# Balancing two batches' 4x4 matrices in one pass of doubled width

## The chip, the core and the metric

The kernel runs on one core of a Trainium2 chip. Its engines are named as in the profile: PE (TensorE; PEld is its weight load), DVE (VectorE), ACT (ScalarE), POOL (GpSimd) and SP (SyncE, which issues DMAs). Each engine runs its own list of instructions in order and waits on semaphores for the others. The metric is the device time of one execution in microseconds; three runs of the kernel before gave a median of 1330.84 us.

## What is computed

Four layers on x of shape (2, 512, 512): 2 batches of 512 tokens with 512 channels. Each layer is

```
xn = layernorm(x)
x  = x + attention_layer(xn) * silu(other_layer(xn))
```

The kernel cuts each batch into four tiles of 128 tokens (T = 512 columns). The attention of layers 0, 2 and 3 has 32 heads of 16, that of layer 1 eight heads of 32; layer 2 is not causal. The part that matters here is the other branch of layer 1. Per token it makes a 4x4 matrix from a projection and balances it (Sinkhorn, 50 rounds), then mixes four streams of 128 channels with it:

```
u = -logsumexp(Z + v, axis=-1)     # rows      } 50 times
v = -logsumexp(Z + u, axis=-2)     # columns   }
H_res = exp(Z + u + v);  H_res = (1 - g) * I + g * H_res
x_mixed = einsum('btij,btjc->btic', H_res, x_streams)
```

The kernel works on exp(Z) and divides by row sums and column sums in turn. One batch has 4 tiles of 128 tokens on the 128 partitions, so its matrices are 4 x 16 = 64 columns of float32, and the sums 16 columns.

## The kernel before

Up to 312 us there are phases of their own: the first normalisation, the projection of layer 0 and its low-rank feed-forward. From there on everything is one woven part (function weave). It is made of stages, each a list of ticks, and a tick issues a few instructions on several engines. Stages stand in strands by letter: a holds the attentions (batch 0 and 1 of layer 0, then of layer 1, 2, 3), b the chain between them (outward product, gate and add, normalise, project, lead of the next attention), c the lead of batch 1's first attention, s the layer-1 branch (class Streams, two stages s0 and s1 for the two batches), r the routed branches of layers 2 and 3, w the splitting of weights on POOL. The string TURNS says in which order the ticks of the strands follow each other ("s12 a" is twelve ticks of s, then one of a), and merge writes one order from it; every engine's list follows that order. Within a strand the order is fixed.

The names in the rows: w_banks are seven PSUM banks that all stages share; w_qs and w_ks hold stacked queries and keys; w_mx the row maxima of the scores (L1402, made by PE at L1259, L1263 and L1271); w_pr the probabilities (scores at L1299, exponentials at L1345, masked on POOL at L1384); w_po the sums over values (L1317); a group of four heads (two in layer 1) ends with L1327, L1410 and L1413. L982, L1008, L667, L1014, L1021 and L1026 are the outward product, its gate and its addition; L718 to L739 the normalisation, L667 and L883, L909 the projection.

Streams has ticks 0 to 12 for logits and exponentials, 13 to 21 for the branch that sums the streams and multiplies by W_branch (L1831 to L1838), 22 to 321 for the balancing (one DVE instruction each, six to a round), three ticks for the gate and 16 for the mixing (L1867, 64 instructions per batch). The balancing steps wait for one another through one semaphore; they read and write columns of w_region. s1 stands behind s0 in its strand, so batch 0's balancing lies under batch 1's first attention and the stages behind it, batch 1's under the layer-1 attentions and the beginning of layer 2's. Batch 0's outward product of layer 1 needs s0's result for its gate, batch 1's needs s1's.

Of the kernel before, what the change touches and what calls it, by code (L numbers as in the profile page):

```python
# [30 lines left out]
P = 128  # L31
D = 512
# [1643 lines left out]
class Streams(Stage):  # L1676


    N, ITERS, INV_TAU, EPS = 4, 50, 10.0, 1.1920929e-07

    def __init__(self, g, b, xn, w24, wb, base, gate, norm, weights):
        self.g, self.b, self.xn, self.w24, self.wb, self.base, self.gate = g, b, xn, w24, wb, base, gate
        self.norm, self.weights = norm, weights
        s = g.signals
        self.squared, self.meaned, self.rooted = s.take("h_squared", NI), s.take("h_meaned", 1), s.take("h_rooted", 1)
        self.gate_exped, self.made = s.take("h_gate_exped", 1), s.take("h_made", 1)
        self.done = s.take("h_done", 13)
        self.centred, self.exped = s.take("h_centred", 2), s.take("h_exped", 2)
        self.balanced = s.take("h_balanced", 6 * self.ITERS)
        self.pre, self.turned, self.hi, self.lo = s.take("h_pre", NI * 4), s.take("h_turned", 1), s.take("h_hi", 1), s.take("h_lo", 1)  # L1690
        self.branched, self.kept = s.take("h_branched", 1), s.take("h_kept", 1)
        self.posted, self.mixed, self.silued = s.take("h_posted", NI), s.take("h_mixed", NI * 16), s.take("h_silued", NI // 2)
        self.pre_at, self.bal_at = 13, 22
        self.gate_at = self.bal_at + 6 * self.ITERS
        self.mix_at = self.gate_at + 3
        self.ticks = range(self.mix_at + NI * 4 + 1)
        self.fills = {}

    def cost(self, t):
        if self.bal_at <= t < self.gate_at:  # L1700
            return 0.28
        return 1.0
# [40 lines left out]
    def act(self, act, t):  # L1743
        g, n = self.g, self.N
        if t < NI:
            act.wait_ge(self.norm.normed.sem, self.norm.normed.at + NI)
            if t == 0:
                wait_pos(act, self.posted.sem, self.posted.at)
                act.activation(g.h_gt[:, 0:1], self.gate, ACT.Exp, scale=-1.0).then_inc(self.gate_exped.sem, 1)
            wait_pos(act, self.squared.sem, self.squared.at + t)  # L1750
            act.activation(g.h_sq[:, :], self.xn[:, t, :], ACT.Square, accum_out=g.h_ss[:, t:t + 1]).then_inc(self.squared.sem, 1)
        if t == 5:
            act.wait_ge(self.meaned.sem, self.meaned.at + 1)
            act.activation(g.h_ss[:, :], g.h_ss[:, :], ACT.Sqrt).then_inc(self.rooted.sem, 1)
        if t == 11:
            act.wait_ge(self.centred.sem, self.centred.at + 2)
            act.activation(g.h_mix[:, :, :], g.h_mix[:, :, :], ACT.Exp, scale=self.INV_TAU).then_inc(self.exped.sem, 1)
            act.activation(g.h_pp[:, :, :], g.h_pp[:, :, :], ACT.Exp).then_inc(self.exped.sem, 1)
# [10 lines left out]
        if t - self.mix_at in (-1, 3, 8, 9):  # L1769
# [3 lines left out]
            for k in range(n):  # L1773
                op = act.activation(g.h_om[:, i % 2, k * P:(k + 1) * P], g.h_sq[:, i * P:(i + 1) * P], ACT.Copy,
                                    scale=g.h_pp[:, i, n + k:n + k + 1])
# [7 lines left out]
    def dve(self, dve, t):  # L1783
        g, n = self.g, self.N
        done = self.done
        if t == 4:
            dve.wait_ge(self.squared.sem, self.squared.at + NI)
            dve.tensor_scalar(g.h_ss[:, :], g.h_ss[:, :], 1.0 / D, self.EPS, ALU.mult, ALU.add).then_inc(self.meaned.sem, 1)
        res = g.h_lg[:, :, 0:n * n].rearrange("p t (i j) -> p t i j", j=n)
        two = g.h_lg[:, :, n * n:].rearrange("p t (i j) -> p t i j", j=n)  # L1790
        two_p = g.h_pp[:, :, :].rearrange("p t (i j) -> p (t i) j", j=n)
        if t == 6:
            dve.wait_ge(self.rooted.sem, self.rooted.at + 1)
            dve.reciprocal(g.h_rr[:, :], g.h_ss[:, :]).then_inc(done.sem, 1)
        elif t == 7:
            dve.wait_ge(self.made.sem, self.made.at + 1)
            dve.wait_ge(done.sem, done.at + 1)
            dve.tensor_tensor(g.h_lg[:, :, :], g.banks.at(self.fills["logits"])[:, 0:NI * 24].rearrange("p (t n) -> p t n", n=24),
                              g.h_rr[:, :].unsqueeze(2).to_broadcast([P, NI, 24]), ALU.mult).then_inc(done.sem, 1)
        elif t == 8:  # L1800
            dve.wait_ge(done.sem, done.at + 2)
            dve.tensor_tensor(g.h_lg[:, :, :], g.h_lg[:, :, :], self.base.unsqueeze(1).to_broadcast([P, NI, 24]),
                              ALU.add).then_inc(done.sem, 1)
        elif t == 9:
            dve.wait_ge(done.sem, done.at + 3)
            dve.tensor_reduce(g.h_m4[:, :], res, AX.X, ALU.max).then_inc(done.sem, 1)
            dve.tensor_reduce(g.h_m2[:, :, :], two, AX.X, ALU.max).then_inc(done.sem, 1)
        elif t == 10:
            dve.wait_ge(done.sem, done.at + 5)
            dve.tensor_tensor(g.h_mix[:, :, :].rearrange("p t (i j) -> p t i j", j=n), res,  # L1810
                              g.h_m4[:, :].rearrange("p (t i) -> p t i", i=n).unsqueeze(3).to_broadcast([P, NI, n, n]),
                              ALU.subtract).then_inc(self.centred.sem, 1)
            dve.tensor_tensor(g.h_pp[:, :, :].rearrange("p t (i j) -> p t i j", j=n), two,
                              g.h_m2[:, :, :].unsqueeze(3).to_broadcast([P, NI, 2, n]), ALU.subtract).then_inc(self.centred.sem, 1)
        elif t == 12:
            dve.wait_ge(self.exped.sem, self.exped.at + 2)
            m2 = g.h_m2[:, :, :].rearrange("p t i -> p (t i)")
            dve.tensor_reduce(m2, two_p, AX.X, ALU.add).then_inc(done.sem, 1)
            dve.wait_ge(done.sem, done.at + 6)
            dve.reciprocal(g.h_i2[:, :], m2).then_inc(done.sem, 1)  # L1820
            dve.wait_ge(done.sem, done.at + 7)
            dve.tensor_tensor(two_p, two_p, g.h_i2[:, :].unsqueeze(2).to_broadcast([P, NI * 2, n]), ALU.mult)\
                .then_inc(done.sem, 1)
        elif self.pre_at <= t < self.pre_at + 4:
# [497 lines left out]
```

## Time and profile before

| | us |
|---|---|
| median of 3 runs (1326.19 to 1334.57) | 1330.84 |
| the profiled execution | 1323.33 |
| its span in the profile | 1321.3 |
| busy PE, DVE, ACT, POOL | 1063.8, 862.6, 581.8, 328.6 |

The span is what the profile shows between the first and the last instruction. Busy times overlap between engines, so they are compared with the span, stage by stage, and not added.

### The profile page before, as it was taken

The numbers are of one execution on the slowest core, as the hardware profiler recorded it, in microseconds if no ns is written. First come the engines' busy times: TensorE is split into PE (matmuls) and PEld (weight loads), VectorE is DVE, ScalarE is ACT, GpSimd is POOL, SyncE is SP. The second block draws the span as 40 slices with busy tenths as digits, with TensorE's granted clock in tenths as the row PEclk, the third lists the DMA queues.
The fourth block names the chain that finished last, engine by engine and source line by source line (L and its number), as shares of the span: only waits on it lengthen the run. The fifth ranks groups of instructions, "written<-read, shape, count | busy, mean of one in ns | idle before, by whom it ended". The sixth has DMA issues, their size and how long they took to land.

```text
span 1321.3 us, 20167 instructions
## 1 busy us (share of the span) xinstructions
PE 1063.8 (81%) x7480; PEld 446.7 (34%) x7480; DVE 862.6 (65%) x1775; ACT 581.8 (44%) x801; POOL 328.6 (25%) x516
## 2 busy tenths in 40 slices
PE   3899999996779677756758666588889987999878
PEld 2444444442234322424323111232223343434424
DVE  5322221003567789989798999957978687757764
ACT  3433333001564643315533366555665666444562
POOL 2145444004653111101121000158310042111230
PEclk9889999997799768878979599788999998999999
DMA  8322220004110001100202000033102111220200
GB/s 314 117 72 72 72 72 0 0 0 104 51 43 17 13 13 31 60 13 15 71 28 79 19 19 19 17 113 111 47 23 82 48 45 34 61 73 29 66 14 32
DMA packets 54901, 69.74 MB, mean 53 GB/s; under 512 B 9526, under 2 KB 43444, under 8 KB 54800
## 3 DMA queue, kind: packets, MB, share of 16 engines
q1 hardware_dynamic: 50828, 58.57, 14.2%
q0 software_dynamic: 3984, 9.98, 2.7%
q8 instruction: 56, 0.92, 0.3%
q14 instruction: 33, 0.27, 0.1%
HBM read 49.45 MB, written 18.82 MB: 52 GB/s over the span
## 4 chain that ended last, share of the span: by engine, by line
DVE 33%; PE 30%; ACT 5%; issue 4%; DMA 3%; SPq 2%; POOL 0%; DVEq 0%; ACTq 0%
DVE w_mx L1402 15%; PE w_banks L667 9%; PE w_po L1317 7%; PE w_banks L1299 4%; PE w_banks L1271 3%; ACT w_pr L1345 2%; PE w_banks L1259 2%; DVE w_region L1867 2%; DVE w_region L1889 2%; PE w_banks L1327 2%; PE w_banks L1553 2%; DMA stack_scratch<-sl_region 1%; DVE w_region L1886 1%; DVE att L1021 1%; DVE w_region L1884 1%
## 5 line engine op out<-in xcount | busy, mean ns | idle before, releaser
L1345 ACT ACTIVATE w_pr<-w_banks 128x1024 f32<-128x1024 f32 (+1 forms) x312 | 313.8, 1014 | 301.9 <-PE w_banks L1299 301.2
L1402 DVE TENSOR_REDUCE w_mx<-w_banks 128x2 f32<-128x1024 f32 (+3 forms) x352 | 373.4, 1082 | 110.0 <-PE w_banks L1271 108.7
L1384 POOL TENSOR_SCALAR_AFFINE_SELECT w_pr<-w_pr 128x512 f32<-128x512 f32 (+1 forms) x184 | 109.2, 595 | 447.0 <-ACT w_pr L1345 446.7
L1299 PE MATMUL w_banks<-w_qs,w_ks 49*128 49x512 f16 (+7 forms) x832 | 134.3, 350 | 64.8 <-ACT w_pr L1345 30.2
L1271 PE MATMUL w_banks<-w_ks,w_qs 48*128 48x512 f16 (+7 forms) x832 | 143.0, 359 | 25.3 <-DVE w_mx L1402 21.8
L78 PE MATMUL f_pp<-xt,sl_region 128*128 128x512 f16 x672 | 149.5, 383 | 2.4 <-POOL sl_region L504 2.4
L1317 PE MATMUL w_po<-w_pr,w_vz 128*17 128x512 f32 (+7 forms) x1152 | 144.2, 538 | 2.1 <-ACT w_ou L1367 2.1
L1259 PE MATMUL w_banks<-mask_half,ident_half 64*128 64x128 bf16 (+1 forms) x768 | 68.6, 259 | 42.9 <-DVE w_mx L1402 25.5
L480 DVE TENSOR_TENSOR sl_region<-sl_region,f_pp 128x512 f32<-128x512 f32 x28 | 19.3, 688 | 120.6 <-ACT sl_region L495 120.6
L78 PEld LDWEIGHTS f_pp<-xt,sl_region 128*128 128x128 f16 x672 | 65.2, 99 | 84.0 <-issue 6.1
L1299 PEld LDWEIGHTS w_banks<-w_qs,w_ks 49*128 49x128 f16 (+1 forms) x832 | 40.8, 99 | 122.1 <-ACT w_pr L1345 55.7
L78 PE MATMUL d_pf<-f_wd,f_dt 128*128 128x512 f16 x336 | 74.3, 385 | 3.7 <-PEq L69 3.7
L1271 PEld LDWEIGHTS w_banks<-w_ks,w_qs 48*128 48x128 f16 (+1 forms) x832 | 47.7, 103 | 86.7 <-DVE w_mx L1402 49.0
L667 PE MATMUL w_banks<-xt,w_region 128*128 128x512 f16 x288 | 70.3, 391 | 5.6 <-DVE w_mx L1402 2.7
L1259 PEld LDWEIGHTS w_banks<-mask_half,ident_half 64*128 64x128 bf16 x768 | 29.3, 99 | 96.0 <-issue 57.1
L667 PE MATMUL w_banks<-w_wo,w_ot 128*128 128x512 f16 x192 | 49.3, 409 | 8.8 <-DVE w_ot L1008 8.8
L1317 PE MATMUL w_po<-w_pr,vz 128*17 128x256 f32 (+3 forms) x512 | 54.9, 508 | 1.2 <-POOL w_pr L1384 0.8
L1442 POOL DMA_DIRECT2D w_stage<-in_L_w x40 | 22.2, 556 | 133.1 <-issue 125.0
L1889 DVE RECIPROCAL w_region<-w_region 128x16 f32<-128x16 f32 x200 | 50.0, 250 | 4.9
L2219 DVE MEMSET w_po<- 128x512 f32 x1 | 0.5, 485 | 78.5 <-PEq L351 78.5
L511 POOL TENSOR_TENSOR f_dt<-sl_region,f_dt 128x512 f32 (+1 forms) x28 | 32.4, 1156 | 69.4 <-ACT f_dt L497 69.4
L78 PEld LDWEIGHTS d_pf<-f_wd,f_dt 128*128 128x128 f16 x336 | 33.2, 99 | 44.8 <-issue 6.3
(223 smaller groups left out, 1487.8 us busy)
## 6 DMA issues: line engine op xcount, KB each, us to landing
stack_scratch<-sl_region SPq DMA_DIRECT2D x102, 128.0 KB
w_qs<-stack_scratch SPq DMA_DIRECT2D x96, 96.0 KB, 2.3
sl_region<-in_L_gu SPq DMA_DIRECT2D x14, 512.0 KB
w_stage<-in_L_w POOLq DMA_DIRECT2D x36, 128.0 KB, 2.4
sl_region<-in_L_down SPq DMA_DIRECT2D x14, 256.0 KB
stack_scratch<-p_qk SPq DMA_DIRECT2D x24, 128.0 KB
w_ks<-stack_scratch SPq DMA_DIRECT2D x32, 96.0 KB, 2.6
bw_stage<-in_L_w SPq DMA_DIRECT2D x4, 640.0 KB, 9.9
```

What stands on the lines that cost most here:

```text
L78: mm = pe.matmul(out, left(a, c), right(b, c), start=first and k == 0, stop=last and k == n - 1)
L511: pool.tensor_tensor(dt[:, 1, ds(i, 1), b * T:(b + 1) * T], sd[:, b:b + 1, :], dt[:, 0, ds(i, 1), b * T:(b + 1) * T], ALU.subtract).then_i ...
L667: mm = pe.matmul(out, left(a, c), right(b, c), start=k == 0, stop=k == len(terms) - 1)
L1259: mm = pe.matmul(out[:, :, keys - P:keys], g.ident_half[64 * half:64 * half + 64, piece, :], g.mask_half[64 * half:64 * half + 64, piece, ...
L1271: mm = pe.matmul(out, g.qs[base:base + self.rows, slot, place, i * P:(i + 1) * P], g.ks[base:base + self.rows, k_slot, k_place, 0:keys], s ...
L1299: mm = pe.matmul(g.banks.pair_at(f)[:, half, at:at + T - q0], g.ks[base:base + self.rows + 1, k_slot, k_place, j * P:(j + 1) * P], g.qs[ba ...
L1317: mm = pe.matmul(g.po[s * a.sw:s * a.sw + a.hd + 1, q0:T], self.vz[:, j, head * a.kv // a.h, :], g.probs.at(self.pr_fill[og * self.n_u + u ...
L1327: mm = pe.transpose(g.banks.at(self.out_fill[og])[:, i * P:(i + 1) * P], g.ou[:, (self.base + og) % 2, i * P:(i + 1) * P], g.ident[:, :])
L1345: act.activation(g.probs.at(self.pr_fill[s])[:, :, 0:width], g.banks.pair_at(self.s_fill[s])[:, :, 0:width], ACT.Exp, scale=self.a.scale). ...
L1384: pool.affine_select(out=diagonal, in_=diagonal, compare_op=ALU.is_ge, fill=0.0, base=0, pattern=pattern, channel_multiplier=-1).then_inc( ...
L1402: dve.tensor_reduce(out, g.banks.pair_at(self.m_fill[m])[:, :, 0:heads * keys].rearrange("q h (p k) -> q h p k", k=keys), AX.X, ALU.max).t ...
L1889: op = dve.reciprocal(inverse, sums)
```

## The change

The balancing is taken out of Streams and becomes a stage of its own (class Balance) that works on both batches: h_mix becomes one tile of 2 x 64 columns, the sums and inverses one of 32, and each of the 300 instructions reads or writes twice the columns. There are 50 rounds in place of two times 50. It begins when both batches' exponentials are there. The strand s now is: s0 to its tick 21, s1 to its tick 12, the balancing, s0's gate and mixing, then s1's branch, gate and mixing. The small tiles of Streams and its semaphores get one copy per batch, and TURNS is a new table for the new strands.

```diff
-    def balance(self, dve, k):
-        g, n = self.g, self.N
-        byrow = g.h_mix[:, :, :].rearrange("p t (i j) -> p (t i) j", j=n)
-        bycol = g.h_mix[:, :, :].rearrange("p t (i j) -> p t j i", j=n)
+class Balance(Stage):
+    def __init__(self, g, streams):
+        self.g, self.streams, self.steps = g, streams, 6 * Streams.ITERS
+        self.balanced = g.signals.take("h_balanced", self.steps)
+        self.ticks = range(self.steps)
...
+    def dve(self, dve, t):
+        g, n = self.g, Streams.N
+        both = g.h_mix[:, :, :, :].rearrange("p b t m -> p (b t) m")
+        byrow = both.rearrange("p t (i j) -> p (t i) j", j=n)
+        bycol = both.rearrange("p t (i j) -> p t j i", j=n)
         sums, inverse = g.h_m4[:, :], g.h_i4[:, :]
-        if k > 0:
-            dve.wait_ge(self.balanced.sem, self.balanced.at + k)
-        step = k % 6
+        if t == 0:
+            for stage in self.streams:
+                dve.wait_ge(stage.exped.sem, stage.exped.at + 2)
+        else:
+            dve.wait_ge(self.balanced.sem, self.balanced.at + t)
+        step = t % 6
         if step == 0:
             op = dve.tensor_reduce(sums, byrow, AX.X, ALU.add)
         elif step == 2:
-            op = dve.tensor_tensor(byrow, byrow, inverse.unsqueeze(2).to_broadcast([P, NI * n, n]), ALU.mult)
+            op = dve.tensor_tensor(byrow, byrow, inverse.unsqueeze(2).to_broadcast([P, NT * n, n]), ALU.mult)
         elif step == 3:
             op = dve.tensor_reduce(sums.rearrange("p (t j) -> p t j", j=n), bycol, AX.X, ALU.add)
         elif step == 5:
             op = dve.tensor_tensor(bycol, bycol, inverse.rearrange("p (t j) -> p t j", j=n).unsqueeze(3)
-                                   .to_broadcast([P, NI, n, n]), ALU.mult)
+                                   .to_broadcast([P, NT, n, n]), ALU.mult)
         else:
             op = dve.reciprocal(inverse, sums)
         op.then_inc(self.balanced.sem, 1)
...
 TURNS = """
...
-    a2 w2 a2 w6 l w2 a2 w a14 w a w a3 w a2 w a2 w2 a w a10 w a2 w2 a w a2 c2 a c3 w a c a3 w c2 a3 c a c a c a c w2
+    w4 a3 w6 a w a12 w a3 w2 a3 w2 a10 w2 a5 w2 a4 w2 a w a2 c a w c w c w c2 l a c a2 c a c2 a3 c a2 c w a w c w a2
...
-                   "s": [all_of(s0), all_of(s1)], "r": [all_of(x) for x in (r20, r21, r30, r31)]}
+                   "s": [some_of(s0, 0, s0.gate_at), some_of(s1, 0, s1.pre_at), all_of(balance),
+                         some_of(s0, s0.gate_at, s0.ticks[-1] + 1), some_of(s1, s1.pre_at, s1.ticks[-1] + 1)], "r": [all_of(x) for x in (r20, r21, r30, r31)]}
```

The first place is DVE where the balancing begins. Before, batch 0's rounds begin there, among the maxima (L1402) of batch 1's first attention:

```order
L1838 TENSOR_TENSOR w_region<-w_banks,w_region 128x512
L1880 TENSOR_REDUCE w_region<-w_region 128x16
L1889 RECIPROCAL w_region<-w_region 128x16
L1882 TENSOR_TENSOR w_region<-w_region 128x64
L1884 TENSOR_REDUCE w_region<-w_region 128x16
L1889 RECIPROCAL w_region<-w_region 128x16
L1886 TENSOR_TENSOR w_region<-w_region 128x4x4x4
```

Now, with the same operations at other lines (L1893 to L1902), behind batch 1's exponentials:

```order
L1817 RECIPROCAL w_region<-w_region 128x8
L1819 TENSOR_TENSOR w_region<-w_region 128x32
L1893 TENSOR_REDUCE w_region<-w_region 128x32
L1902 RECIPROCAL w_region<-w_region 128x32
L1895 TENSOR_TENSOR w_region<-w_region 128x128
L1897 TENSOR_REDUCE w_region<-w_region 128x32
L1902 RECIPROCAL w_region<-w_region 128x32
L1899 TENSOR_TENSOR w_region<-w_region 128x8x4x4
```

Every row has twice the columns, and the first of them has moved from among batch 1's first attention to behind its normalisation.

The second place is DVE near the end of the balancing and behind it. Before, batch 1's last rounds stood among the maxima of layer 2's attention for batch 0:

```order
L1402 TENSOR_REDUCE w_mx<-w_banks 128x2
L1880 TENSOR_REDUCE w_region<-w_region 128x16
L1889 RECIPROCAL w_region<-w_region 128x16
L1882 TENSOR_TENSOR w_region<-w_region 128x64
L1402 TENSOR_REDUCE w_mx<-w_banks 128x2
L1884 TENSOR_REDUCE w_region<-w_region 128x16
L1889 RECIPROCAL w_region<-w_region 128x16
L1402 TENSOR_REDUCE w_mx<-w_banks 128x2
L1886 TENSOR_TENSOR w_region<-w_region 128x4x4x4
L1402 TENSOR_REDUCE w_mx<-w_banks 128x2
```

Now that attention's first maxima stand behind the projection (L883, L909) and the last mixes (L1862, which was L1867), with no balancing among them:

```order
L883 SCALAR_TENSOR_TENSOR sl_region<-w_banks,bw_cols,sl_region 128x512 x3
L909 TENSOR_TENSOR w_vz<-w_banks,bw_rows 128x32x16
L1862 SCALAR_TENSOR_TENSOR w_region<-sl_region,w_region 128x128 x32
L1592 COPY w_r_l<-w_banks 128x16
L1402 TENSOR_REDUCE w_mx<-w_banks 128x2 x12
L1592 COPY w_r_l<-w_banks 128x16
L1402 TENSOR_REDUCE w_mx<-w_banks 128x2
```

The layer-2 attention has moved from beside the balancing to behind it. Between the first and the last balancing step DVE now has 37 other instructions: 21 maxima (L1402), four pairs of L1410 and L1413, four L883, two L909 and two L1008, all of layer 1.

## Rows read from the trace of the kernel before

**Rows 1.** The page, busy us, share of the span, instructions.
```profile
PE 1063.8 (81%) x7480; PEld 446.7 (34%) x7480; DVE 862.6 (65%) x1775; ACT 581.8 (44%) x801; POOL 328.6 (25%) x516
```
**Rows 2.** Windows: stretch and length, busy us by engine, granted clock, DMA share, GB/s.
```profile
312.70:411.70 99.00, 74.84 (x827) 30.60 (x827) 63.76 (x76) 49.00 (x59) 62.87 (x123) 0.84 0.24 64
465.00:720.00 255.00, 183.31 (x1250) 85.10 (x1250) 224.41 (x717) 96.45 (x147) 40.52 (x69) 0.82 0.12 38
720.00:846.00 126.00, 76.93 (x455) 18.91 (x456) 120.03 (x291) 64.35 (x85) 1.35 (x3) 0.82 0.07 20
846.00:909.00 63.00, 50.76 (x337) 19.93 (x335) 43.79 (x69) 37.41 (x48) 38.38 (x70) 0.92 0.32 96
909.00:1060.00 151.00, 136.16 (x867) 45.46 (x866) 118.32 (x157) 88.05 (x113) 28.55 (x53) 0.98 0.19 56
1060.00:1318.00 258.00, 229.06 (x2009) 100.39 (x2007) 177.94 (x280) 129.53 (x164) 54.97 (x99) 0.98 0.15 44
```
**Rows 3.** Groups by line and form on DVE: count, busy us, mean ns, idle before.
```profile
L1889 DVE RECIPROCAL w_region<-w_region 128x16 f32<-128x16 f32 x200 | 50.0, 250 | 4.9
L1886 DVE TENSOR_TENSOR w_region<-w_region 128x64 f32<-128x64 f32 x100 | 27.0, 270 | 2.7
...
L1882 DVE TENSOR_TENSOR w_region<-w_region 128x64 f32<-128x64 f32 x100 | 23.4, 234 | 2.6
...
L1802 DVE TENSOR_TENSOR w_region<-w_region,w_base 128x96 f32<-128x96 f32 x2 | 0.5, 259 | 0.1
...
L1810 DVE TENSOR_TENSOR w_region<-w_region 128x64 f32<-128x64 f32 x2 | 0.4, 224 | 0.1
...
L1820 DVE RECIPROCAL w_region<-w_region 128x8 f32<-128x8 f32 x2 | 0.4, 204 | 0.1
...
L1794 DVE RECIPROCAL w_region<-w_region 128x4 f32<-128x4 f32 x2 | 0.4, 178 | 2.7 <-ACT w_region L1754 2.7
```
**Rows 4.** Timeline of DVE: start us, us, line, operation.
```profile
565.82 0.27 DVE L1886 TENSOR_TENSOR w_region<-w_region 128x64 f32<-128x64 f32 x1
...
567.51 0.27 DVE L1886 TENSOR_TENSOR w_region<-w_region 128x64 f32<-128x64 f32 x1
...
605.22 8.49 DVE L1867 SCALAR_TENSOR_TENSOR w_region<-sl_region,w_region 128x128 f32<-128x128 f32 x32
```
**Rows 5.** The chain that ended last, first attention: start us, us, what.
```profile
338.44 2.37 DVE w_mx L1402 x2
...
350.16 2.37 DVE w_mx L1402 x2
360.20 2.37 DVE w_mx L1402 x2
```
**Rows 6.** Windows of 10 us within the first attention, columns as in rows 2.
```profile
334.00:344.00 10.00, 8.50 (x63) 2.28 (x61) 4.07 (x5) 4.14 (x5) 5.13 (x11) 0.50 0.13 34
364.00:374.00 10.00, 7.33 (x97) 3.04 (x93) 6.57 (x9) 5.78 (x8) 3.43 (x7) 1.00 0.12 33
```
**Rows 7.** Groups by line and form on PE: count, busy us, mean ns, idle.
```profile
L667 PE MATMUL w_banks<-xt,w_region 128*128 128x512 f16 x288 | 70.3, 391 | 5.6 <-DVE w_mx L1402 2.7 <-ACT w_mn L1360 2.6 <-DVE xt L739 0.3
L667 PE MATMUL w_banks<-w_wo,w_ot 128*128 128x512 f16 x192 | 49.3, 409 | 8.8 <-DVE w_ot L1008 8.8
...
L982 PE MATMUL w_banks<-ident,att 128*128 128x128 f32 x112 | 19.6, 304 | 9.8 <-DVE att L1413 8.1 <-POOL w_tables L1457 1.1 <-DVE w_mx L1402 0.6
```
**Rows 8.** Timeline of DVE at four places.
```profile
428.92 0.69 DVE L1014 TENSOR_TENSOR att<-w_banks,w_o_rows 128x512 f32<-128x512 f32 x1 [0.40 <-PE w_banks L667]
...
458.04 0.86 DVE L1831 TENSOR_SCALAR w_region<-sl_region,w_region 128x128 f32<-128x128 f32 x4
...
719.04 0.69 DVE L909 TENSOR_TENSOR w_vz<-w_banks,bw_rows 128x512 f32<-128x512 f32 x1 [0.93 <-PE w_banks L667]
...
1317.15 0.69 DVE L1026 TENSOR_TENSOR x_res<-x_res,att 128x512 f32<-128x512 f32 x1
```
**Rows 9.** Windows, the instructions of L1889 alone: length, DVE busy, clock, DMA share.
```profile
720.00:823.00 103.00, 11.83 (x48) 0.85 0.09 24
```

More of the change, by code:

```diff
@@ L1783, in dve @@
     def dve(self, dve, t):
-        g, n = self.g, self.N
-        done = self.done
+        g, b, n = self.g, self.b, self.N
+        done, m4 = self.done, g.h_m4[:, b * 16:(b + 1) * 16]
         if t == 4:
             dve.wait_ge(self.squared.sem, self.squared.at + NI)
[L1788 to L1791, printed above, removed]
+            dve.tensor_scalar(g.h_ss[self.b][:, :], g.h_ss[self.b][:, :], 1.0 / D, self.EPS, ALU.mult, ALU.add).then_inc(self.meaned.sem, 1)
+        res = g.h_lg[self.b][:, :, 0:n * n].rearrange("p t (i j) -> p t i j", j=n)
+        two = g.h_lg[self.b][:, :, n * n:].rearrange("p t (i j) -> p t i j", j=n)
+        two_p = g.h_pp[self.b][:, :, :].rearrange("p t (i j) -> p (t i) j", j=n)
         if t == 6:
             dve.wait_ge(self.rooted.sem, self.rooted.at + 1)
-            dve.reciprocal(g.h_rr[:, :], g.h_ss[:, :]).then_inc(done.sem, 1)
+            dve.reciprocal(g.h_rr[self.b][:, :], g.h_ss[self.b][:, :]).then_inc(done.sem, 1)
         elif t == 7:
@@ L1912 @@
+    a2 b r9 b2 r4 a r b7 a3 b3 a r a r a r a2 b2 a r2 a r2 b2 a r2 a b r b r2 a b r b r4 a b2 a r b2 a b7 a b a2 b3
+    a3 b2 a2 b a2 b a3 b a3 r2 a2 r2 a3 r a r2 a3 r a r5 a r2 a r9 a r a5 r5 a2 r a r a3 r3 a3 r a r8 a r b r2 b r2
+    b2 r2 b16
 """
@@ L1948, in body_of, with some_of @@
     return stage, range(0, stage.ticks[-1] + 1)
+def some_of(stage, first, last):
+    return stage, range(first, last)
 class Shared:
@@ L2076, in weave @@
     g.h_xpt, g.h_sq = view(region, 4608, (2, T), F16), view(region, 5120, (D,), F32)
-    g.h_mix, g.h_pp, g.h_lg = (view(region, at, (NI, n), F32) for at, n in ((5632, 16), (5696, 8), (5728, 24)))
-    g.h_m4, g.h_i4 = view(region, 5824, (16,), F32), view(region, 5840, (16,), F32)
-    g.h_m2, g.h_i2 = view(region, 5856, (NI, 2), F32), view(region, 5864, (8,), F32)
-    g.h_ss, g.h_rr, g.h_gt = (view(region, at, (n,), F32) for at, n in ((5872, 4), (5876, 4), (5880, 3)))
+    g.h_mix, g.h_m4, g.h_i4 = (view(region, 5632, (NB, NI, 16), F32), view(region, 5760, (NB * 16,), F32),
+                               view(region, 5792, (NB * 16,), F32))
+    g.h_pp, g.h_lg, g.h_m2, g.h_i2, g.h_ss, g.h_rr, g.h_gt = (
+        [view(region, at + b * size, shape, F32) for b in range(NB)]
+        for at, size, shape in ((5824, 32, (NI, 8)), (5888, 96, (NI, 24)), (6080, 8, (NI, 2)), (6096, 8, (8,)),
+                                (6112, 4, (4,)), (6120, 4, (4,)), (6128, 4, (3,))))
     wo1, w24 = view(tables, 0, (2, 2, D), F16), view(tables, 1024, (2, KC, 24), F16)
```

113 lines of the change are left out of this document (53 added, 60 removed).

## The prediction

> **What bounds the kernel now.** I read the page first, then the busy time of each engine by stage, then the Sinkhorn rows, then one period of the first attention, last the chain of waits. The page [rows 1] shows no single bound: PE 81%, DVE 65%, ACT 44% of 1321.3 us, and the 40 slices show PE high where DVE is low and the reverse. By stage [rows 2] the woven part (from 312.7 us) falls into three kinds. While batch 0's first attention runs alone (312.7 to 411.7) PE is busy 74.84 of 99 us and DVE 63.76: neither is full. From 465 to 846 DVE is busy 224.41 + 120.03 = 344 of 381 us (90%) and PE only 260: DVE is the bound, and these are the stages where the two batches' balancing runs. From 909 on PE is the bound (136.16 of 151, 229.06 of 258).
>
> **One round of balancing.** A round is six dependent steps. Where nothing stands between them the column-wise multiply starts at 565.82 and again at 567.51 [rows 4]: 1.69 us a round, hand-overs included, 169 us for the 100 rounds. After the change there are 50, with twice the columns in each.
>
> **What a wider round costs.** Slopes come from rows of other widths [rows 3]. Multiply: 64 columns 224 ns, 96 columns 259 ns, so 1.1 ns a column, and 64 columns more cost about 67 ns; the row-wise reduction is taken the same. The column-wise multiply is 36 ns dearer than the row-wise one at 64 columns (270 against 234); whether that is fixed or grows is not shown, so it and the column-wise reduction get +67 to +103 each; I take +85. Reciprocal: 4 columns 178, 8 columns 204, 16 columns 250, so 5.8 to 6.5 ns a column; these rows are close to 32, so +95 for each of the two, with +17 (1.1 ns a column, as the multiply) as the lower end and +104 as the upper. Sum: 67 + 67 + 2 x 85 + 2 x 95 = 494 ns, a round of 2.18 us, 109 us for 50. DVE saves 169 - 109 = **60 us**. Between the ends a round is 1.99 to 2.24 us, 100 to 112 us.
> That the reciprocal is dearer per column than the rest is what the rows say. The Trainium skill, VectorE: DVE Perf Modes (section The DVE is not a fixed-function vector unit), names an iterative divide with a repeat count of 8. Read as eight cycles a column that is an estimate of 8.3 ns, a reciprocal of 383 ns, and the round would be 2.26 us, the saving 56 us; the trace's rows give less, and the sum goes by the rows.
>
> **What the move costs.** The 60 us are worth their full time only where DVE stays the bound, and the new order changes what stands beside the balancing. It can start only when both batches' matrices are there, so behind the whole of batch 1's first attention, its outward product and its normalisation. I follow the new order in four stretches; before, they end at 411.7, 465, 720 and 1317.8.
>
> *a) To the first balancing step.* Batch 0's attention is unchanged: 411.7. Batch 1's first attention now has only matmul stages beside it. Its eight groups of heads take 10.05 us each where nothing disturbs them [rows 5], with PE busy 7.33 and DVE 6.57 of 10 [rows 6]: 80.4 us with 21 us of free PE. Put between them in the new order: 80 matmuls of the outward products (49.3/192 = 0.257 each, 20.6), 48 of 512 columns of the projection (70.3/288 = 0.244, 11.7) and 48 of 256 (half of that, 5.9), 48 transposes (19.6/112 = 0.175, 8.4), and some 6 us of small products: 52 us [rows 7]. 80.4 + 52 - 21 = 111; I take 113 (105 to 125, the lower end is all of it at PE's busy sum less a fifth of overlap). Behind it the serial tail outward, normalise, logits, exponentials, which before ran from 428.92 to 458.04 [rows 8], 29 us. First balancing step at 411.7 + 113 + 29 = **554** (before: 465, for batch 0 alone).
>
> *b) The balancing.* 109 us of rounds, and between them in the new order only 37 other DVE instructions of the small layer-1 attention and its projection, 25 us by their rows: 21 maxima at about 0.9 (two of the widest take 2.37 [rows 5]), the rest 0.2 to 0.7. A few tenths go back where one runs into the next. 132 us, end at **686**. PE has about 43 us of work here: it is idle two thirds of the stretch. That is the price of the change.
>
> *c) To the end of batch 0's layer-2 projection* (before: 719.04 + 0.69 = 719.7 [rows 8]). A serial chain: mix, Silu, gate, normalise, project; DVE fills its holes with batch 1's mixing. DVE work: 96 mixes at 8.49/32 = 0.27 [rows 4], 26, 16 of the pre-mix 5, twelve 512-column adds and multiplies 8.5, normalise 8, projection 5, attention rests 3, some 3 small: 58 us, with three table loads and hand-overs 62. End at **748**, 28 us later than before.
>
> *d) The rest.* From the same point before needs 1317.8 - 719.7 = 598 us [rows 8]. Its first 126 us (720 to 846) were filled by DVE, 120 busy, with 48 reciprocals of 24 balancing rounds in 103 us [rows 9]; these rounds with the remaining mixes (64 x 0.27 = 17, of which 9 stay) take about 24 x 1.69 + 8 = 49 us away. What is left is DVE 71 and PE 77 us of work, about even. Stretches in which the two are near each other ran at a PE share of 0.81 (846 to 909) and 0.90 (909 to 1060) [rows 2]: 95 or 86 us. I take 86, the larger stretch: saved 40. 598 - 40 = 558, end at 748 + 558 = **1306** against 1317.8.
>
> So -12 us: of 60 us saved on DVE some 48 are given back, since PE idles under an uncovered chain. The profiled execution had 1323.3 us, 7.5 below the median of 1330.84; I put the difference on the median: 1330.8 - 12 = **1319 us**. Within 1% (13 us) is about what a measurement of this kernel can tell from no change.
>
> Costed at nothing: the renamed semaphores and the moved columns of the region (the instructions of the batches' own parts keep engine and shape); the weight splitting of layer 3, which moves earlier by one stage, on POOL, which is busy 1.35 of 126 us there [rows 2]; if its cover went, it would cost the projection of layer 3 a wait of a few us. SP's queue keeps the same transfers in another place; the stores and loads ahead of the layer-2 attention, which lay under balancing, now lie under the last 32 mixes (9 us) alone: they are next to be late.
>
> **Rivals.**
> *A, most of the saving arrives (chance 0.2).* For it: DVE is the bound from 465 to 846, and stretch d could run at the share of DVE seen there (0.95), 71/0.95 = 75 in place of 86; stretch a at its lower end, 105; the round at 1.99 us. -11 - 8 - 9 on top of -12: -40, 1291 us. Against: all three are ends, not middles.
> *B, slower (0.2).* One mechanism: with the rounds gone from beside it, the layer-2 attention falls into the hand-over pace of the first attention, where DVE is busy only 6.57 of 10 us [rows 6] while PE has time free. The head of stretch d then takes 71/0.657 = 108 us, and with its share of matmul stages 115: 11 saved in place of 40, so -12 + 29 = +17, 1348 us. It decides from 98 us on (28 saved). For it: that pace stands for seven groups in the trace. Against: two strands run there, and 909 to 1060 shows them filling each other.
> *C, TensorE's clock eats the rest (0.1).* In 334 to 344 us the granted clock was 0.50 (the 1.2 GHz level) and the period was 11.7 us (338.44 to 350.16), against 10.05 at 1.00 [rows 5, 6]. PE idles two thirds of b, so it comes out of it at the low level. If it stays there for four such periods, 4 x 1.7 = 7 us: -5, 1326 us. The Trainium skill, TensorE: Matmul & The Clock Gate (section Part 1: The HAM clock gate), says that an idle array falls back to half rate and has to earn the full one again; the rows agree in direction, and by that rule alone the change would end within 1%.
>
> **Chances and range.** The main case (0.5) carries its own range, -30 to +6 (round -9 or +3, stretch a -8 to +12, d -8 to +9, not all at once): 0.22 of it beyond -13, 0.28 within. A adds 0.2 faster, B 0.2 slower, C 0.1 within. Faster 0.42, within 1% 0.38, slower 0.20. The range reaches to both rivals and leaves 0.1 out on either side: 1294 to 1346.
>
> **What would show it.** The reciprocal of 32 columns near 345 ns and a round near 2.2 us. First wide reduction near 554 us, last multiply near 686 with PE busy a third between. The projection's end near 748, the last add near 1306. Wrong if the attention beside the outward product takes more than 125 us, or if DVE and PE both stay under 80% behind 748.

## The result, and the profile after

The change made the kernel slightly slower: 1337.43 us against 1328.05 us (medians of 20 runs each), a ratio of 1.0063 with the 95% interval 1.004 to 1.0087. Forecast were 1319 us and a gain. The profiled execution took 1341.78 us, 4 above its own median, the one of before 1323.33, 5 below; so the two profiles stand some 9 us further apart (18.7 us) than the kernels do, and the stretches below are read with that in mind.

The first line of the page after, which answers to [rows 1]:

```profile
PE 1067.4 (80%) x7480; PEld 447.2 (33%) x7480; DVE 836.0 (62%) x1475; ACT 575.6 (43%) x797; POOL 331.9 (25%) x516
```

DVE has 300 instructions fewer and is busy 836.0 instead of 862.6 us: 26.6 us less, not the 60 of the forecast. (The 60 also held the short hand-overs between dependent steps, in which DVE isn't busy.) Windows of the profile after, for [rows 2]: the rest of batch 1's first attention; the tail up to the first balancing step; the balancing; to the end of batch 0's layer-2 projection; the head of the layer-2 attention; the rest. The columns are those of rows 2.

```profile
415.60:531.60 116.00, 95.28 (x921) 43.31 (x918) 76.54 (x129) 61.59 (x85) 28.35 (x52) 0.94 0.11 34
531.60:566.80 35.20, 27.50 (x190) 16.43 (x187) 24.95 (x52) 16.82 (x30) 1.38 (x3) 0.86 0.04 12
566.80:707.10 140.30, 69.94 (x317) 29.02 (x317) 122.22 (x339) 24.44 (x41) 8.10 (x17) 0.65 0.08 26
707.10:773.30 66.20, 38.67 (x226) 19.53 (x223) 54.15 (x169) 25.09 (x45) 12.67 (x14) 0.78 0.06 19
773.30:930.00 156.70, 120.85 (x746) 34.89 (x743) 126.56 (x176) 88.74 (x116) 61.03 (x108) 0.86 0.25 74
930.00:1336.50 406.50, 364.22 (x2875) 144.41 (x2875) 295.68 (x436) 222.11 (x279) 64.21 (x113) 0.98 0.15 44
```

While the balancing runs, PE is busy 69.94 of 140.30 us, where the forecast had 43 us of work for it, and its granted clock is 0.65; DVE is busy 87%. The groups of the balancing on DVE after, by line and form, for [rows 3]:

```profile
L1902 DVE RECIPROCAL w_region<-w_region 128x32 f32<-128x32 f32 x100 | 35.2, 352 | 3.2
L1899 DVE TENSOR_TENSOR w_region<-w_region 128x128 f32<-128x128 f32 x50 | 19.5, 391 | 1.4
L1897 DVE TENSOR_REDUCE w_region<-w_region 128x32 f32<-128x128 f32 x50 | 18.7, 375 | 1.5
L1895 DVE TENSOR_TENSOR w_region<-w_region 128x128 f32<-128x128 f32 x50 | 14.8, 295 | 1.6
L1893 DVE TENSOR_REDUCE w_region<-w_region 128x32 f32<-128x128 f32 x50 | 14.2, 285 | 1.6
```

The timeline of DVE gives the length of a wide round, from one row-wise reduction to the next, for [rows 4]; and the last of the projection and the last addition, for [rows 8]:

```profile
605.46 0.29 DVE L1893 TENSOR_REDUCE w_region<-w_region 128x32 f32<-128x128 f32 x1
...
607.71 0.29 DVE L1893 TENSOR_REDUCE w_region<-w_region 128x32 f32<-128x128 f32 x1
...
772.63 0.69 DVE L909 TENSOR_TENSOR w_vz<-w_banks,bw_rows 128x512 f32<-128x512 f32 x1 [0.54 <-PE w_banks L667]
...
1335.80 0.69 DVE L1026 TENSOR_TENSOR x_res<-x_res,att 128x512 f32<-128x512 f32 x1
```

| checkpoint, us from the span's start | forecast | after |
|---|---|---|
| one wide round | 2.18 | 2.25 |
| reciprocal of 32 columns | 0.345 | 0.352 |
| first balancing step | 554 | 566.8 |
| last balancing step ends | 686 | 707.1 |
| projection ends (stretch c) | 748 | 773.3 |
| last addition | 1306 | 1336.5 |

The reciprocal and the row-wise steps cost what was forecast. The two column-wise steps grew by more than the range allowed (the multiply from 270 to 391 ns, +121 against +67 to +103), so the round lies just above its upper end of 2.24 us. The reciprocal estimate of 383 ns, set beside the sum in the prediction, was too high; that its round of 2.26 us comes close to 2.25 is luck. Every stretch is longer than forecast, 30.5 us in all. Some 9 us of that are the two profiled executions themselves, one above and one below its median; between the medians the forecast missed by 20 us (8 us lost, -12 forecast).

### The profile page after: what moved, and what is told of

Read it like the earlier page. It is cut to its first block, busy times and chain, and to the rows that moved or that the text cites. A ratio compares the mean times of both kernels' runs of the same rounds, so it can differ in the third digit from the quotient of the medians.

```text
span 1340.1 us, 19853 instructions
## 1 busy us (share of the span) xinstructions
PE 1067.4 (80%) x7480; PEld 447.2 (33%) x7480; DVE 836.0 (62%) x1475; ACT 575.6 (43%) x797; POOL 331.9 (25%) x516
## 4 chain that ended last, share of the span: by engine, by line
PE 32%; DVE 30%; ACT 5%; DMA 3%; issue 3%; POOL 2%; SPq 2%; ACTq 0%; DVEq 0%; POOLq 0%
DVE w_mx L1402 13%; PE w_banks L667 8%; PE w_po L1317 8%; PE w_banks L1271 4%; PE w_banks L1299 3%; DVE w_region L1902 2%; PE w_banks L1259 2%; DMA stack_scratch<-sl_region 2%; PE w_banks L1327 2%; PE w_banks L1553 2%; DVE w_region L1862 2%; ACT w_pr L1345 1%; DMA w_ks<-stack_scratch 1%; DVE w_region L1899 1%; DVE w_region L1897 1%
## 5 line engine op out<-in xcount | busy, mean ns | idle before, releaser
L1402 DVE TENSOR_REDUCE w_mx<-w_banks 128x2 f32<-128x1024 f32 (+3 forms) x352 | 374.2, 1086 | 136.3 <-PE w_banks L1271 134.0
L1271 PE MATMUL w_banks<-w_ks,w_qs 48*128 48x512 f16 (+7 forms) x832 | 144.2, 355 | 30.2 <-DVE w_mx L1402 18.1
L1317 PE MATMUL w_po<-w_pr,w_vz 128*17 128x512 f32 (+7 forms) x1152 | 149.4, 545 | 7.1 <-POOL w_pr L1384 4.6
L1271 PEld LDWEIGHTS w_banks<-w_ks,w_qs 48*128 48x128 f16 (+1 forms) x832 | 47.8, 102 | 98.2 <-DVE w_mx L1402 51.2
L1317 PE MATMUL w_po<-w_pr,vz 128*17 128x256 f32 (+3 forms) x512 | 51.8, 481 | 3.7 <-POOL w_pr L1384 3.7
L667 PE MATMUL w_banks<-w_wo,w_ot 128*128 128x512 f16 x192 | 45.0, 380 | 3.4 <-DVE w_ot L1008 1.9
L1317 PEld LDWEIGHTS w_po<-w_pr,w_vz 128*17 128x17 f32 (+1 forms) x1152 | 24.4, 100 | 67.0 <-issue 52.5
L495 ACT ACTIVATE sl_region<-f_pp 128x512 f32<-128x512 f32 x28 | 16.7, 597 | 69.5 <-PE f_pp L78 69.5
```

Source lines behind the costliest of these rows:

```text
L667: mm = pe.matmul(out, left(a, c), right(b, c), start=k == 0, stop=k == len(terms) - 1)
L1271: mm = pe.matmul(out, g.qs[base:base + self.rows, slot, place, i * P:(i + 1) * P], g.ks[base:base + self.rows, k_slot, k_place, 0:keys], s ...
L1317: mm = pe.matmul(g.po[s * a.sw:s * a.sw + a.hd + 1, q0:T], self.vz[:, j, head * a.kv // a.h, :], g.probs.at(self.pr_fill[og * self.n_u + u ...
L1402: dve.tensor_reduce(out, g.banks.pair_at(self.m_fill[m])[:, :, 0:heads * keys].rearrange("q h (p k) -> q h p k", k=keys), AX.X, ALU.max).t ...
```

## The experiments

Times below are ratios to the kernel before, measured on the same chip, with 95% intervals; us behind them are the change of the ratio times 1328.

**What DVE's time was worth before.** In `balance` of the kernel before, 18 of each batch's 50 rounds are left out, evenly spread (KEPT is 32; the waits are counted anew to fit):

```diff
-        if k > 0:
-            dve.wait_ge(self.balanced.sem, self.balanced.at + k)
-        step = k % 6
+        before, step = k // 6 * self.KEPT // self.ITERS, k % 6
+        if (k // 6 + 1) * self.KEPT // self.ITERS == before:
+            return
...
```

> The kernel before with 32 of its 50 rounds per batch, left out evenly over the 50, so 36 narrow rounds of 1.69 us are missing: 60.8 us less of DVE, about what the change takes from DVE, with every other instruction in its old place (18 rounds per batch of the reference are not done). Theory 1, DVE's load is what this order waits for (it is busy 90% from 465 to 846 us): 0.8 to 0.95 of it arrives, -49 to -58, 1270 to 1279 us; the change then loses over 55 us by its new place. Theory 2, the saving was never worth that much, since PE and the hand-overs take over as soon as DVE is lighter: -20 to -35, 1293 to 1308 us.

Measured: 0.9777 (0.9731 to 0.9823), -30 us. 60.8 us of rounds are worth 30. The page's first line shows why it is less than it looks:

```profile
PE 1058.8 (82%) x7480; PEld 446.6 (34%) x7480; DVE 816.7 (63%) x1559; ACT 581.0 (45%) x801; POOL 327.1 (25%) x516
```

DVE's busy time fell by 862.6 - 816.7 = 45.9 us, and two thirds of that arrived. The other 15 us of the 60.8 are two things of about equal size: hand-overs inside the rounds, which aren't busy time (36 x 0.21 = 7.5 us), and overlap that goes with the rounds left out, so that the instructions beside them count in full (some 7 us; summed over the two traces the overlap fell by 5.7). Theory 2, that the saving was never worth its length, stands.

**The same in the new order.** The same edit in `Balance.dve` of the changed kernel, with KEPT = 23:

> The changed kernel with 23 of its 50 wide rounds, left out evenly: 27 x 2.23 = 60.2 us less of DVE (27 rounds of the reference are not done). The same amount of DVE time as in the run before this one, taken from the other order. Theory 1, the balancing is a bare chain here that everything behind it waits for: all of it arrives, -57 to -60 against the changed kernel's 1337, 1277 to 1280 us. Theory 2, PE's 70 us and the layer-1 attention inside the stretch take over: -40 to -48, 1289 to 1297 us.

Measured: 0.9707 (0.9664 to 0.975); against the changed kernel's 1.0063 that is -47 us of 60.2. In the new order nearly four fifths of a microsecond of balancing arrive, before it was half. That is the upper end of theory 2 (-40 to -48) and not theory 1, the bare chain (-57 to -60). By the two traces the stretch of the balancing became 51 us shorter (140.3 to 88.9), so some 9 us of the rounds left out didn't even shorten the stretch; what filled them was not taken apart.

**The width alone.** Batch 0's columns only, so that batch 1's matrices stay unbalanced (the sums, inverses and broadcasts are narrowed with it):

```diff
-        both = g.h_mix[:, :, :, :].rearrange("p b t m -> p (b t) m")
+        both = g.h_mix[:, 0, :, :]
...
```

> The changed kernel with its 300 steps in their places, but on batch 0's 64 columns alone (batch 1's matrices stay unbalanced). The round goes from 2.23 to 1.69 us: 27 us less. This is what the doubled width costs in the new order. Theory 1 (bare chain): -25 to -27, 1310 to 1312 us. Theory 2 (something else sets the end of the stretch): -12 to -20.

Measured: 0.9908 (0.9875 to 0.9941), -21 us of the 28 by which its round is shorter (1.69 against 2.25 us, 50 times): a rate of three quarters, nearly that of a23, and a value between the two theories, just beyond the end of theory 2 (-20).

**The move without the merging.** Every step is issued once for each batch:

```diff
+        for b in range(NB):
+            one = g.h_mix[:, b, :, :]
...
+                dve.wait_ge(self.balanced.sem, self.balanced.at + 2 * t + b - 1)
```

> The changed kernel's order, but each of the 300 steps issued twice, once for each batch's 64 columns: the move without the merging. DVE's work is that of the kernel before, 100 narrow rounds. Two rounds side by side take 2 x 1.69 = 3.4 us, or 3.0 if the hand-overs inside a round (6 x 0.035) vanish because neighbours no longer depend on each other. Theory 1: 50 x (3.0 to 3.4 less 2.23) = +38 to +58 against the changed kernel, 1375 to 1395 us, so the move alone costs 47 to 67 us against the kernel before and the merging gives that back but for 9. Theory 2 (part of the stretch waits for PE anyway): +25 to +35.

Measured: 0.996 (0.9923 to 0.9997), 1321 us. Both theories were wrong by 40 us and more: with all 600 narrow instructions back it is 1% faster than the wide form, and 0.4% faster than the kernel before, though that interval only just ends below 1. One round of both batches, from the trace of this run, DVE; a row "x2" is two neighbours, one for each batch, the second started under the first:

```profile
597.51 0.42 DVE L1897 TENSOR_REDUCE w_region<-w_region 128x16 f32<-128x64 f32 x2
597.86 0.36 DVE L1902 RECIPROCAL w_region<-w_region 128x16 f32<-128x16 f32 x2
598.14 0.43 DVE L1899 TENSOR_TENSOR w_region<-w_region 128x64 f32<-128x64 f32 x2
598.47 0.35 DVE L1893 TENSOR_REDUCE w_region<-w_region 128x16 f32<-128x64 f32 x2
598.74 0.37 DVE L1902 RECIPROCAL w_region<-w_region 128x16 f32<-128x16 f32 x2
599.03 0.35 DVE L1895 TENSOR_TENSOR w_region<-w_region 128x64 f32<-128x64 f32 x2
599.29 0.42 DVE L1897 TENSOR_REDUCE w_region<-w_region 128x16 f32<-128x64 f32 x2
```

From 597.51 to 599.29 is 1.78 us for both batches; the wide round took 2.25, two narrow ones in turn 3.38. The row-wise reductions of both batches, 0.22 us each, together take 0.35 us. Over the whole run the second of two such reductions starts 127 ns after the first (median of 50), while a step that needs its predecessor starts 253 ns after it (median of 67 in the kernel before). The other steps show the same in the same two runs: two reciprocals of 16 columns 159 ns apart, a dependent step 287 ns behind one; two column-wise reductions 172 ns, a dependent step 296 ns. So about half of a narrow step's time is latency that an independent neighbour can use. The Trainium skill, VectorE: DVE Perf Modes (sections The DRAIN you can't avoid and Rules for kernel authors), says of chained DVE operations to minimise their count and not the semaphores, since the pipeline drains after each anyway (for a next operation that nothing holds it names an earlier start, without a time); by that rule 600 instructions must lose to 300. The runs show the opposite, 1321 against 1337 us, and they decide.

**The move at the old pace.** As a_two, but a round of batch 0 is issued whole before that of batch 1, so that every step waits for the one before it ("-" is a_two):

```diff
-        for b in range(NB):
+        for x in range(2 * t, 2 * t + 2):
+            b = x // 6 % 2
...
-                dve.wait_ge(self.balanced.sem, self.balanced.at + 2 * t + b - 1)
+                dve.wait_ge(self.balanced.sem, self.balanced.at + x)
```

> The order and the instructions of a_two (300 narrow steps for each batch, in the change's place), but a round of batch 0 is issued whole before the round of batch 1 instead of side by side, so that each step again waits for the one before it. This is the move with rounds at the old pace. Theory L: two rounds take 3.38 us instead of 1.79, +80 us in the stretch of the balancing, of which 0.75 to 0.85 arrives as in the runs with fewer columns and fewer rounds: +60 to +68 against a_two's 1321, 1381 to 1389 us. Then the move costs some 55 us by itself and what pays for it is the latency hidden, by width or by neighbours. Theory T, a_two was quick since the new table is better everywhere and the pace of the steps matters little: within 15 us of a_two.

Measured: 1.0482 (1.0449 to 1.0515), 1387.91 us, +64 against before and 67 above a_two, as theory L has it. The instructions are the same 600 (one line further down in this file); only their order and the waits that go with it differ. Timeline of DVE:

```profile
606.17 0.22 DVE L1894 TENSOR_REDUCE w_region<-w_region 128x16 f32<-128x64 f32 x1
606.43 0.25 DVE L1903 RECIPROCAL w_region<-w_region 128x16 f32<-128x16 f32 x1
606.71 0.23 DVE L1896 TENSOR_TENSOR w_region<-w_region 128x64 f32<-128x64 f32 x1
```

And the page of a_seq, first line:

```profile
PE 1071.8 (77%) x7480; PEld 448.9 (32%) x7480; DVE 884.4 (64%) x1775; ACT 575.5 (41%) x797; POOL 324.3 (23%) x516
```

DVE is busy 884.4 us, 22 more than in the kernel before with the same 1775 instructions. In the old order a good part of the steps had an independent instruction behind them that started under their latency, as here at 575.30 (the neighbour starts after 0.14 us, where the dependent step at 578.19 starts after 0.26), kernel before:

```profile
575.30 0.22 DVE L1880 TENSOR_REDUCE w_region<-w_region 128x16 f32<-128x64 f32 x1
575.44 0.68 DVE L1014 TENSOR_TENSOR att<-w_banks,w_o_rows 128x512 f32<-128x512 f32 x1
...
577.93 0.22 DVE L1880 TENSOR_REDUCE w_region<-w_region 128x16 f32<-128x64 f32 x1
578.19 0.25 DVE L1889 RECIPROCAL w_region<-w_region 128x16 f32<-128x16 f32 x1
```

By count, 161 of the 600 steps of the kernel before are followed by another line's instruction, at some 115 to 120 ns less each than a dependent one: 19 us. In the new order there are few strangers to put there (31 of 300 steps, and 31 of 600 in a_seq). Summed over the whole run, DVE's instructions overlap by 74 us in the kernel before and by 59 us in a_seq; these 15 us are most of the 22. The rest are instructions that lasted a little longer.

**Hiding latency in the old order.** Each narrow step of the kernel before as two independent halves of two token tiles:

```diff
+        for c in range(2):
+            part = g.h_mix[:, c * half:(c + 1) * half, :]
...
+                dve.wait_ge(self.balanced.sem, self.balanced.at + 2 * k + c - 1)
```

> The kernel before in its own order, but each balancing step is issued as two independent halves of two token tiles each (32 columns, sums of 8), so every second instruction depends on nothing that is still running. Theory L, the pace of a step is the latency of a dependent instruction: the traces show 253 ns from one dependent 64-column step to the next and 127 ns where the next is independent; a column is worth 1.06 ns (253 against 321 ns at 128 columns), a reciprocal's 6.3 ns. Two halves are then issued in about 190 ns and the dependent one waits 219: the round goes from 1.69 to 1.45 us, 24 us less of DVE's time over 100 rounds; at the rate at which 36 left-out rounds paid in this order (30 of 60.8 us) that is -12: 1315 us. Theory C, the cost is in the number of instructions (about 200 ns each whatever their width and neighbour): a round of 12 takes 2.4 us, +70 of DVE, +35 to +60: 1362 to 1387 us.

Measured: 0.9971 (0.9951 to 0.9991), -4 us. The undisturbed round did shorten to 1.41 us (median of 23), even more than theory L said; its pairs of halves follow each other every 0.22 to 0.24 us:

```profile
564.63 0.30 DVE L1882 TENSOR_REDUCE w_region<-w_region 128x8 f32<-128x32 f32 x2
564.85 0.32 DVE L1891 RECIPROCAL w_region<-w_region 128x8 f32<-128x8 f32 x2
565.09 0.31 DVE L1884 TENSOR_TENSOR w_region<-w_region 128x32 f32<-128x32 f32 x2
```

```profile
PE 1071.2 (81%) x7480; PEld 450.9 (34%) x7480; DVE 869.9 (66%) x2375; ACT 582.6 (44%) x801; POOL 327.9 (25%) x516
```

But only a third of the expected gain arrived, and DVE's busy time rose by 7 us: where a stranger already stood behind a step, there was no latency left to hide and the second half is extra. That last reason was not measured apart, but the miss fits the reading: in the old order a round must not be priced by its undisturbed length.

**Is it the table?** TURNS was searched anew, with the instructions unchanged, for a_two and for the kernel before; the order found for a_two was used again with the wide steps. The first line of a_tuned's table against the changed kernel's:

```diff
 TURNS = """
-    w4 a3 w6 a w a12 w a3 w2 a3 w2 a10 w2 a5 w2 a4 w2 a w a2 c a w c w c w c2 l a c a2 c a c2 a3 c a2 c w a w c w a2
...
+    w a w a10 w a w5 a3 w2 a3 w a2 w a w2 a7 w a3 w2 a2 w2 a w a9 w2 a c2 w a c a c2 a w a2 c a l w c2 w a c a3 w2
...
```

> The instructions of a_two with another TURNS (order of the ticks alone), found by a search over orders that replays the five queues with the durations of the traces. If the 9 us that the change lost were owed to a table that does not fit it, a better one must beat both kernels: -15 to -30 against a_two, 1291 to 1306 us. If the end is set by the chain through the balancing and by the sums of DVE and PE behind it, order does little: within 8 us of a_two.

> The kernel before with another TURNS, found by the same search, its instructions unchanged: 100 dependent narrow rounds in their old stages. It tells whether what a_tuned wins belongs to the new structure. If old and new structure are worth the same once each has its order: 1295 to 1305 us, within 8 us of a_tuned. If the place of the balancing is what limits the new one, b_tuned is the quicker by 15 or more; if the shared rounds are the better structure, it is the slower by 10 or more.

> The changed kernel's wide steps (128 columns in one instruction) in the order of a_tuned, so the only difference from a_tuned is one wide instruction in place of two narrow ones side by side: a round of 2.25 in place of 1.79 us, 23 us over 50 rounds. Theory L: 0.7 to 0.8 of it shows, as between the changed kernel and a_two (16 us): 1293 to 1298 us. Theory T, in an order that fits, other work covers the balancing: within 6 us of a_tuned's 1278.

| kernel | its given order | its searched order |
|---|---|---|
| before, 100 dependent rounds | 1 | 0.9822 (0.9796 to 0.9848) |
| the change, 50 wide rounds | 1.0063 (1.004 to 1.0087) | 0.9777 (0.9758 to 0.9796) |
| 50 rounds of narrow pairs | 0.996 (0.9923 to 0.9997) | 0.9661 (0.9631 to 0.9691) |

a_tuned, 1277.97 us, beats both kernels and my expectation of it. Width costs the same in either order: 1.0063 - 0.996 and 0.9777 - 0.9661 are both 1%, 14 to 15 us. And the merged structure, once each has an order that fits, is no loss: the wide form stands 0.45% (6 us) below b_tuned, with intervals that just touch. So the 8 us that the change lost belong in part to its table. b_tuned stands 25 us above a_tuned, so of its three cases the last holds: shared rounds are the better structure, as far as one search for each tells; a longer search could shift either. What a_tuned gains on a_two lies mostly behind the projection. Windows of a_tuned (balancing; to the projection's end; the rest), then of b_tuned (first balancing step to the projection's end; the rest), the ends within 0.6 us:

```profile
551.90:667.00 115.10, 67.61 (x349) 28.08 (x348) 111.93 (x636) 26.82 (x45) 11.49 (x24) 0.74 0.10 29
667.00:739.10 72.10, 35.97 (x207) 19.00 (x206) 64.49 (x206) 26.32 (x51) 2.33 (x5) 0.76 0.12 36
739.10:1273.70 534.60, 479.92 (x3606) 178.40 (x3604) 409.46 (x577) 305.10 (x383) 122.23 (x221) 0.96 0.17 52
```

```profile
454.90:702.50 247.60, 183.08 (x1364) 89.66 (x1361) 226.52 (x711) 100.22 (x152) 32.89 (x67) 0.87 0.13 39
702.50:1297.60 595.10, 501.99 (x3632) 183.09 (x3629) 462.55 (x811) 318.38 (x407) 121.79 (x223) 0.91 0.16 48
```

The rest takes 534.6 us in a_tuned against 563.2 in the changed kernel; in the kernel before it is 598 and stays 595. Which moves in the table give these 28 us was not taken apart.

**Masks held back by the mixing.** In the changed kernel's chain of waits, 7 us of POOL stand behind the balancing, a mask made while DVE mixes. Timeline after, POOL, DVE and PE's weight load:

```profile
708.14 8.49 DVE L1862 SCALAR_TENSOR_TENSOR w_region<-sl_region,w_region 128x128 f32<-128x128 f32 x32
...
709.99 7.86 POOL L1384 TENSOR_SCALAR_AFFINE_SELECT w_pr<-w_pr 128x512 f32<-128x512 f32 x3 [2.68 <-ACT w_pr L1345]
...
717.18 0.19 PEld L1317 LDWEIGHTS w_po<-w_pr,w_vz 128*33 128x33 f32 x4 [5.25 <-POOL w_pr L1384]
```

```diff
             if t == self.mix_at:
                 dve.wait_ge(done.sem, done.at + 13)
+                if b == 0:
+                    dve.wait_ge(self.beside.masked.sem, self.beside.masked.at + 10)
```

> The changed kernel with one wait more: DVE begins batch 0's mixing only when POOL has made the masks that it made under the mixing before (three masks took 7.86 us there, 0.4 to 0.6 each elsewhere). Theory P, the mixing holds POOL's instruction back until it ends: the masks take 0.6 us each again, the attention beside it ends some 5 us sooner, ScalarE's Silu 2 to 4 us sooner, DVE loses about 4 us of waiting: 1331 to 1337 us, no gain beyond that. Theory Q, the long masks are slow for a reason of their own (a table, a queue): they still take over 5 us and the time is 3 to 5 us longer.

Measured: 1.0085 (1.006 to 1.0109), no different from the change's 1.0063. The timeline of this run (the mixing is at L1864 in it):

```profile
704.30 0.64 POOL L1384 TENSOR_SCALAR_AFFINE_SELECT w_pr<-w_pr 128x512 f32<-128x512 f32 x1 [2.75 <-ACT w_pr L1345]
705.45 0.41 POOL L1384 TENSOR_SCALAR_AFFINE_SELECT w_pr<-w_pr 128x256 f32<-128x256 f32 x1 [0.51 <-ACT w_pr L1345]
...
707.47 9.04 DVE L1864 SCALAR_TENSOR_TENSOR w_region<-sl_region,w_region 128x128 f32<-128x128 f32 x32 [5.12 <-POOL w_pr L1384]
...
709.04 0.85 POOL L1384 TENSOR_SCALAR_AFFINE_SELECT w_pr<-w_pr 128x512 f32<-128x512 f32 x1 [1.66 <-ACT w_pr L1345]
...
710.19 0.41 POOL L1384 TENSOR_SCALAR_AFFINE_SELECT w_pr<-w_pr 128x256 f32<-128x256 f32 x1 [0.30 <-ACT w_pr L1345]
```

Made ahead of the mixing, the masks take 0.64 and 0.41 us again, as theory P has it; but DVE waits 5.12 us for them, and nothing is won on balance. The last two rows show more than the theory asked for: two further masks start under the mixes of this run and take only 0.85 and 0.41 us, while the mixing takes 9.04 us in place of 8.49. So the mixing can hold a mask for its whole length, but doesn't always. In a_seq, too, five masks get in between the mixes, at 0.41 to 0.86 us each. And it is no new cost of the change: in the kernel before a mask that starts at 608.40 us, under batch 0's mixing, takes 5.58 us. The Trainium skill, SBUF — State Buffer (section SBUF: two separate sides), has the rule: a DVE instruction with two SBUF inputs and a GpSimd instruction that reads SBUF exclude each other. The traces agree in both cases: after, the first of the three masks lasts 7.14 us, until the last mix has ended; in a_wait a mix beside a mask lasts 0.72 us in place of 0.34. What decides which of the two waits, no run here shows.

## Why the prediction was wrong

- **The failed step is the price of the move: "of 60 us saved on DVE some 48 are given back".** Measured apart, the new place and table with rounds at the old pace cost +64 us (a_seq), not 48. The width then brings 1.0482 - 1.0063, 56 us, where I had 60. Of the 20 us by which the forecast missed, 16 are the move and 4 the width. In the sum for 1306 us the move is the four stretches, and each was too short, as said below for each. What place and table cost each by itself was not measured.
- **"DVE saves 60 us" was wrong for the old order**, though its price of an old round enters the sum only in stretch d, as 24 x 1.69. It took both rounds by their undisturbed length [rows 4]. The wide side was nearly right (2.25 against 2.18 us). The old side was not: those rounds stood among other instructions that ran under their latency. The two rows that [rows 3] leaves out:

```profile
L1884 DVE TENSOR_REDUCE w_region<-w_region 128x16 f32<-128x64 f32 x100 | 26.1, 261 | 2.5
L1880 DVE TENSOR_REDUCE w_region<-w_region 128x16 f32<-128x64 f32 x100 | 21.7, 217 | 2.5
```

  With them the balancing's own rows fell from 148.2 to 102.4 us, 45.8, and the idle time before the steps from 15.2 to 9.3. But DVE's whole busy time fell by 26.6 us only, since other instructions had overlapped with the old steps: about 33 us of DVE's time came free. b32 shows the same without the change: 60.8 us by the clean round, 45.9 by the page, 30 in the result. The lost overlap also stands in the price of the move, as 22 us of busy time in a_seq.
- **Stretch a (+9 us beside a start 4 us later).** The attention took 116 us for my 113. Behind it I counted 29 us, which in the old tail begin only with the addition at 428.92. From the addition on the new tail took less, 20.5 us, but ahead of it I had left out the end of the outward product, whose last 48 matmuls stand behind the last heads: together 35.2 us. The chain of waits after shows these 14.6 us, from 531.6 to 546.2:

```profile
532.47 0.87 PE w_banks L982 x4
533.36 0.61 ACT w_ot L1000
533.99 0.70 DVE w_ot L1008
534.69 0.14 issue
534.82 2.75 PE w_banks L667 x12
537.57 0.44 PE w_banks L982 x4
538.01 2.59 PE w_banks L667 x12
540.60 0.44 PE w_banks L982 x4
541.04 5.19 PE w_banks L667 x24
```

  Not all of it is the kernel: the five other runs with the same order and instructions up to there begin the balancing at 560.8 to 565.9 us, the profiled execution after at 566.8. So 7 to 13 us are missing here.
- **Stretch b (+8).** 50 x 0.07 = 3.5 us come from the wider round, the rest from maxima that DVE waits for (PE at L1271, some 7 us within the stretch) with a balancing step queued behind them. I had costed only their busy time, and PE's work at 43 us, where the window has 69.94. How much of that is the lower clock was not taken apart.
- **Stretch c (+4).** The masks held under the mixing were not in it; a_wait, without them, still took 65.0 us there (after: 66.2), and its DVE waited instead. The rest stays open.
- **Stretch d (+5).** 563 us against 558 forecast and 598 before: the 40 us credited were nearly there (35). It is 560 to 566 us in a23, a_one and a_two as well, so this step was sound. The 5 us may be the price of the old round again: of the 143 balancing steps behind 719.7 us in the kernel before, 56 had a stranger behind them, an estimate of 6 to 7 us at 115 to 120 ns each.
- **Rivals.** The sign was that of B, the mechanism was not: the head of the layer-2 attention ran with DVE busy 81% (126.56 of 156.70 us), not 66%. C did not decide either. The granted clock was 0.65 in the balancing (0.82 in rows 2 from 465 us) and fell to 0.50 once behind it, from 784 to 796 us; but the kernel before has such a stretch too, from 736 to 748 us, and over its head (720 to 909 us) the same mean of 0.86. PE's busy time rose by 3.6 us in all. That the clock costs nothing is not shown by this. A rival was missing altogether: that the old rounds cost less than they look.
- **The range** (1294 to 1346) held the time; the forecast itself, a gain, was wrong.

## What to carry to other kernels

Before a chain of small DVE instructions is made wider or shorter, look at what stands behind each of its steps in the trace: where an independent instruction follows, the latency is already hidden, and the group's count times its undisturbed pace overstates what it costs. Two independent chains are better issued side by side than fused into wider instructions, where latency is about half of a step (here 1.78 us a round against 2.25). And a structure that moves work must be judged with an order that fits it: the same instructions moved by 3% with the table alone.

## What the runs showed of the hardware

- Two row-wise reductions of 64 columns on DVE that don't depend on each other start 127 ns apart (a_two), a step that depends on one 253 ns behind it (before); for column-wise reductions it is 172 and 296 ns. With 128 columns a step that depends on a row-wise reduction starts 321 ns behind it (after; 1.06 ns a column), with 32 columns independent steps are 110 to 124 ns apart (b_half). Behind a reciprocal the dependent step starts after 288 ns at 16 columns and 388 at 32 (6.3 ns a column).
- An instruction on POOL that meets a row of back-to-back mixes on DVE can be held until they end: the first mask took 7.14 us after, 5.58 before, 5.12 to 6.47 in the runs a23, a_one and a_two. It can also get in between: 0.85 us in a_wait, where the mix beside it took 0.72 us in place of 0.34.
- The changed kernel's own 20 runs spread from 1328.91 to 1344.90 us with the mean granted clock: of the four at 0.905 and 0.906 three took 1329 to 1330 us and one 1334.78, the five at 0.899 took 1335 to 1342.
